# First attention of a Trainium2 kernel: two score passes interleaved unit by unit, row sums turned on TensorE, scores from two parts instead of three

## The chip, the cores and the metric

The kernel runs on one core of a Trainium2 chip. Its time is the device time of one execution in microseconds (us). TensorE multiplies matrices (PE is its multiply side, PEld its weight load), VectorE is DVE, ScalarE is ACT, GpSimd is POOL, and SyncE (SP) issues most DMAs.

## The reference

The whole is four transformer layers on x (8 batches, 256 rows, width 256), each an attention and a feed-forward sublayer after a layer norm. The change touches the first attention alone; q is the normalised x, k and v are a context of the same size.

```
qh = (q @ Wq.T + bq)  -> 16 heads of width 16      # kh, vh the same from the context
scores = einsum('bhqd,bhkd->bhqk', qh, kh) / sqrt(16)
scores = where(mask == 0, -1e10, scores);  attn = softmax(scores)
out = einsum('bhqk,bhkd->bhqd', attn, vh) -> (B, S, 256);  x = x + out @ Wo.T + bo
```

## The kernel before

The function `attention0` (lines 166 to 563) works batch by batch, eight batches of 256 rows. Each engine has its own program and waits on semaphores; PE runs its program in order. A unit `u` is two heads, so a batch has U = 8 units. Scores are formed twice. The first pass (`scores`, line 324) has queries on the partitions, and DVE takes the row maxima (`maxima`, line 517). The second pass (`weigh`, line 350) has keys on the partitions, takes the maxima in as further rows of the product, and ACT takes exp into `pT`; that is the layout in which the product with V needs it.

Full precision of the scores comes from three bf16 parts of q and of k (high, middle, low), stacked by DMA so that six products of parts are one contraction over 96 rows (`PARTS`, `to_stack`, line 223). SP issues the 12 DMAs for q and POOL the 12 for k; DVE makes the parts with ACT (`split`, `prepare`). The mask is added by a product of a bf16 identity with a tile of 0 or -2^100 (lines 340 and 365), one for each 128x256 piece of scores.

Both passes use the same four PSUM banks (0 to 3), two banks a unit, so they can't run at once. PE's order in a batch b (line 395) is: `project(b+1)` (q, k, v projections in fp32), `weigh(b)` in which unit u of the second pass alternates with the product of unit u-1 with V (line 376, four fp32 matmuls into 32 columns each, two column groups at a time), `scores(b+1)`, `spread_sums(b)`, `turn_maxima(b+1)`, `output(b)`. The softmax sums are a column of ones in V. `turn_sums` on SP moves them by DMA across the partitions, DVE inverts them (`reciprocals`), DMA moves them back into `rrow`, and a 128x128 selector product (line 384) spreads them over the partitions. DVE then multiplies (`onorm`, line 550), PE applies Wo, DVE adds to x (line 557).

The maxima go the way PE transpose (347), ACT, DVE, ACT, DVE (three parts, 457 to 532), three DMAs (263), and only then can `weigh` of that batch start. The loop is a hardware loop over pairs of batches (`every_batch`), with the last two batches written out.

Of the kernel before, what the change touches and what calls it, by code (L numbers as in the profile page):

```python
# [21 lines left out]
P = 128  # L22
# [143 lines left out]
def attention0(nc, top, x, xt, io, consts):  # L166

    G, NG, W = 4, H // 4, 32
    U = H // 2
    PARTS = ((0, 0, 0, 1, 1, 2), (0, 1, 2, 0, 1, 0))
    R = len(PARTS[0]) * D0  # L180
    LAND = 16 * 2 * len(PARTS[0])
    HB = P // D0
    with top.stage() as ctx:
        def sb(name, shape, dt=F32):
# [6 lines left out]
        sel = sb("sel", [P, P])  # L191
        ctxT = sb("ctxT", [P, 2, DK, S])
        mask, maskT = sb("mask", [P, TB, S], I32), sb("maskT", [P, TB, S], I32)
        neg, negT = sb("neg", [P, 2, TB, S], BF16), sb("negT", [P, 2, TB, S], BF16)
        part = sb("part", [P, 3, 2, DK, S], BF16)
        rest = sb("rest", [P, 2, DK, S])
        qs, ks = sb("qs", [P, 2, H, S], BF16), sb("ks", [P, 2, H, S], BF16)
        V = sb("V", [P, 2, TB, H, W])
        top_s = sb("top_s", [P, TB, H])
        mpart, mrest = sb("mpart", [H, 3, S], BF16), sb("mrest", [H, S])  # L200
        pT = sb("pT", [P, 2, 2, TB, S])
        sums, recip = sb("sums", [P, NG * S // W]), sb("recip", [P, NG * S // W])
        rrow = sb("rrow", [P, NG, S])
        oraw, onorm = sb("oraw", [P, NG, S]), sb("onorm", [P, NG, S])
        ps = ctx.enter_context(nc.psum_tensor("a0_ps", [P, 8, 512], F32))
        O = ps[:, 4:6, :].rearrange("p a (c n) -> p (a c) n", c=2)

        (weights, ctx_in0, ctx_in1, mask_in, ones_set, q_proj, k_proj, v_proj, hi_done, rest_done, mid_done, lo_done,
         stacked, v_out, neg_ready, s_ready, max_done, mt_ready, mhi_done, mrest_done, mmid_done, mlo_done,
         mrow_landed, st_ready, exp_done, pv_done, o_out, sums_landed, recip_landed, l_ready, recip_done, norm_done,  # L210
         wo_ready, resid_done) = (
             top.semaphore("a0_" + n) for n in (
                 "weights", "ctx_in0", "ctx_in1", "mask_in", "ones_set", "q_proj", "k_proj", "v_proj", "hi_done",
                 "rest_done", "mid_done", "lo_done", "stacked", "v_out", "neg_ready", "s_ready", "max_done",
                 "mt_ready", "mhi_done", "mrest_done", "mmid_done", "mlo_done", "mrow_landed", "st_ready",
                 "exp_done", "pv_done", "o_out", "sums_landed", "recip_landed", "l_ready", "recip_done", "norm_done",
                 "wo_ready", "resid_done"))
        gate, gate_set = sb("gate", [1, 4]), top.semaphore("a0_gate_set")
# [4 lines left out]
        def to_stack(engine, w, n, s):  # L223

            for t, which in enumerate(PARTS[w]):
                if which == n:
                    for k in range(DK):
                        engine.dma_start((qs, ks)[w][t * D0:(t + 1) * D0, s, k * HB:(k + 1) * HB, :],
                                         part[:, n, w, k, :]).then_inc((stacked, k_stacked)[w], 16)

        def every_batch(engine, body):

            with engine.Fori(0, B // 2 - 1) as pair:
                body(pair * 2, 0, pair, False)
                body(pair * 2 + 1, 1, pair, False)
            body(B - 2, 0, B // 2 - 1, False)
            body(B - 1, 1, B // 2 - 1, True)

        @block.sync
        def _(sp):  # L240
            sp.sem_inc(stacked, 16)
            sp.sem_inc(mrow_landed, 16)

            def load(b, s):
                sp.wait_ge(v_proj, b + 1)
                sp.dma_start(ctxT[:, s, :, :], io["ctxT"][bass.ds(b, 1)].rearrange("b (k p) s -> p (b k) s", p=P)
                             ).then_inc(ctx_in[s], 16)
                sp.wait_ge(neg_ready, b + 1)
                sp.dma_start(mask[:, :, :], io["mask"][bass.ds(b, 1)].rearrange("b (t p) s -> p (b t) s", p=P)
                             ).then_inc(mask_in, 16)  # L250
                sp.dma_start(maskT[:, :, :], io["maskT"][bass.ds(b, 1)].rearrange("b (t p) s -> p (b t) s", p=P)
                             ).then_inc(mask_in, 16)

            def stack(b, s):

                for n, ready in enumerate((hi_done, mid_done, lo_done)):
                    sp.wait_ge(ready, b * 2 + 1)
                    to_stack(sp, 0, n, s)

            def shift_rows(b, s):  # L260
                sp.wait_ge(mlo_done, b + 1)
                for n in range(3):
                    sp.dma_start(qs[R + n:R + n + 1, s, :, :], mpart[:, n, :]).then_inc(mrow_landed, 16)

            def turn_sums(b):

                sp.wait_ge(o_out, b * 2 + 2)
                for g in range(G):
                    sp.dma_start(sums[g * W:(g + 1) * W, :], oraw[g * W + D0:g * W + D0 + 1, :, :]
                                 ).then_inc(sums_landed, 16)  # L270
                sp.wait_ge(recip_done, b + 1)
                for g in range(G):
                    sp.dma_start(rrow[g * W + D0:g * W + D0 + 1, :, :], recip[g * W:(g + 1) * W, :]
                                 ).then_inc(recip_landed, 16)

            def feed(b, s):

                sp.wait_ge(pv_done, b * U + 2)
                stack(b + 1, 1 - s)
                turn_sums(b)  # L280
                shift_rows(b + 1, 1 - s)

            for dst, name in ((wq, "a0_wq"), (wk, "a0_wk"), (wv, "a0_wv"), (wo, "a0_wo")):
                sp.dma_start(dst[:, :, :], io[name].rearrange("k p n -> p k n")).then_inc(weights, 16)
            sp.dma_start(bqk[:, :, :], io["a0_bqk"]).then_inc(weights, 16)
            for dst, name in ((bv, "a0_bv"), (sel, "a0_sel")):
                sp.dma_start(dst[:, :], io[name]).then_inc(weights, 16)
            load(0, 0)
            load(1, 1)
            stack(0, 0)  # L290
            shift_rows(0, 0)
            with sp.Fori(0, B // 2 - 1) as pair:
                for s in range(2):
                    load(pair * 2 + (2 + s), s)
                    feed(pair * 2 + s, s)
            feed(B - 2, 0)
            turn_sums(B - 1)

        @block.tensor
        def _(pe):  # L300
            pe.sem_inc(v_proj, 2)
            pe.sem_inc(pv_done, 2)
            pe.sem_inc(l_ready, 1)
            pe.sem_inc(wo_ready, 1)
            pe.wait_ge(weights, 16 * 7)

            def project(b, s, half, left=1):
                pe.wait_ge(ctx_in[s], half * 16 + 16)
                pe.wait_ge(norm_done, left)
                for n, (w, src, done) in enumerate(((wq, xt, q_proj), (wk, ctxT, k_proj))):  # L310
                    for c in range(DK):
                        for k in range(DK):
                            mm = pe.matmul(ps[:, 6 + n, c * S:(c + 1) * S], w[:, k, c * P:(c + 1) * P],
                                           xt[:, k, bass.ds(b * S, S)] if src is xt else ctxT[:, s, k, :],
                                           start=(k == 0), stop=(k == DK - 1))
                    mm.then_inc(done, 1)
                pe.wait_ge(rest_done, b * 2 + 1)
                for t in range(TB):
                    for k in range(DK):
                        mm = pe.matmul(ps[:, 6, t * S:(t + 1) * S], ctxT[:, s, k, t * P:(t + 1) * P], wv[:, k, :],  # L320
                                       start=(k == 0), stop=(k == DK - 1))
                mm.then_inc(v_proj, 1)

            def scores(b, s, before):

                pe.wait_ge(stacked, (b + 1) * LAND + 16)
                pe.wait_ge(k_stacked, (b + 1) * LAND)
                pe.wait_ge(neg_ready, b + 2)
                pe.wait_ge(ones_set, 5)
                for u in range(U):  # L330
                    if u >= 2:
                        pe.wait_ge(max_done, b * U + (u - 1))
                    elif before is not None:
                        pe.wait_ge(exp_done, before * U + (U - 1 + u))
                    for j in range(2):
                        h, bank = 2 * u + j, ps[:, 2 * (u % 2) + j, :]
                        for t in range(TB):
                            pe.matmul(bank[:, t * S:(t + 1) * S], qs[0:R, s, h, t * P:(t + 1) * P], ks[0:R, s, h, :],  # L338
                                      start=True, stop=False)
# [1913 lines left out]
```

## Time and profile before

| | us |
|---|---|
| median of 3 runs (lowest, highest) | 2055.79 (2051.05, 2058.91) |
| the profiled execution's own time | 2057.15 |
| its span in the trace | 2055.3 |
| busy over the span: PE, PEld, DVE, ACT, POOL | 1573.8, 1345.9, 876.4, 550.3, 336.8 |

A row of the list of groups has line, engine, operation, output and input names, shapes, count, then busy time and mean ns of one, then the idle time of the engine before them with what released it. A busy time is the union of intervals; the duration of one matmul is longer than the distance from one to the next, since they are pipelined. In the timeline the first number is the start in us from the span's start, the second the length of the merged row.

### The profile page before, as it was taken

To read this page: it belongs to the slowest core of one execution; us is meant where nothing else is said; L and a number is where in the kernel's file an instruction comes from. 1 tells how busy PE (TensorE), PEld (TensorE's weight loads), DVE (VectorE), ACT (ScalarE), POOL (GpSimd) and SP (SyncE) were. 2 spreads that over 40 slices of the span, in tenths; PEclk is the share of its full clock that TensorE was granted. 3 is DMA by queue.
4 is the path that set the end of the run, shared out by engine and by line. 5 is a ranking of instruction groups with operands and counts; after the bars stand their busy time and mean duration, and the time that the engine had idled before them with its cause. 6 is when DMAs were issued, how large, how long until landed. Compare 5 with 4: busy or idle time off the path is not lost. (4 is left out here: it accounts for less than half of the span.)

```text
span 2055.3 us, 32700 instructions
## 1 busy us (share of the span) xinstructions
PE 1573.8 (77%) x11346; PEld 1345.9 (65%) x11346; DVE 876.4 (43%) x1913; ACT 550.3 (27%) x1311; POOL 336.8 (16%) x401
## 2 busy tenths in 40 slices
PE   2799997539991799999994099999999256691775
PEld 2565664429991688888874099999999244581664
DVE  5443542402224566665665011111111235448896
ACT  1233232102221455454441011111111011231553
POOL 1121120030002333332321400000000511004122
PEclk8999999569996799999995599999999678795787
DMA  4344241158132100000003454224470210101000
GB/s 127 59 76 66 48 69 12 59 200 276 39 113 86 61 7 7 7 7 2 2 1 113 148 195 148 103 67 146 148 270 18 76 47 16 34 26 41 6 15 21
DMA packets 118240, 152.13 MB, mean 74 GB/s; under 512 B 15360, under 2 KB 101376, under 8 KB 118016
## 3 DMA queue, kind: packets, MB, share of 16 engines
q1 hardware_dynamic: 101536, 123.86, 19.6%
q0 software_dynamic: 7680, 18.89, 4.1%
q10 hardware_dynamic: 8928, 8.13, 1.1%
q8 instruction: 56, 0.92, 0.2%
q14 instruction: 40, 0.33, 0.1%
HBM read 113.16 MB, written 24.64 MB: 67 GB/s over the span
## 5 line engine op out<-in xcount | busy, mean ns | idle before, releaser
L1271 PEld LDWEIGHTS f_ph<-f_xgT,f_w 128*128 128x128 f32 x3232 | 373.0, 193 | 21.7 <-issue 18.8
L1271 PE MATMUL f_ph<-f_xgT,f_w 128*128 128x128 f32 x3232 | 374.4, 277 | 16.1 <-DMA f_w<-in_f_w 14.9
L1281 PE MATMUL f_py<-f_w,f_hT 128*128 128x256 f32 x992 | 224.6, 379 | 0.0
L1281 PEld LDWEIGHTS f_py<-f_w,f_hT 128*128 128x128 f32 x992 | 183.7, 190 | 22.6 <-issue 0.2
L1342 DVE TENSOR_TENSOR f_hT<-f_ph,f_gate_o 128x512 f32<-128x512 f32 x78 | 54.0, 692 | 309.3 <-ACT f_gate_o L1305 309.3
L1376 POOL DMA_INDIRECT c_yt<-sorted_y,dest x48 | 45.6, 950 | 649.7 <-issue 648.8
L799 ACT ACTIVATE a_work<-a_ps,a_bias 128x128 f32<-128x128 f32 (+1 forms) x256 | 104.1, 419 | 149.0 <-DVE a_bias L879 91.3
L937 POOL TENSOR_TENSOR a_work<-a_work,a_recip 128x256 f32<-128x256 f32 (+1 forms) x128 | 103.1, 827 | 234.3 <-DVE a_recip L894 234.3
L145 PE MATMUL n_tp<-ident,n_xn 128*128 128x128 f32 x160 | 33.1, 384 | 134.9 <-DVE n_xn L125 134.3
L1305 ACT ACTIVATE f_gate_o<-f_ph 128x512 f32<-128x512 f32 x78 | 46.6, 597 | 295.2 <-PE f_ph L1271 295.1
L145 PEld LDWEIGHTS n_tp<-ident,n_xn 128*128 128x128 f32 x160 | 25.8, 196 | 142.7 <-DVE n_xn L125 135.9
L1260 PE MATMUL f_px<-ident,f_xg 128*128 128x128 f32 x124 | 24.3, 278 | 90.4 <-DMA f_xg<-sorted_x 90.4
L523 DVE TENSOR_REDUCE a_top_s<-a_ps 128x4 f32<-128x1024 f32 x64 | 75.7, 1215 | 16.4 <-PE a_ps L340 15.7
L899 DVE TENSOR_TENSOR a_qk<-a_ps,a_qk 128x512 fp32r<-128x512 f32 x64 | 44.3, 692 | 85.1 <-ACT a_qk L818 85.1
L467 ACT ACTIVATE a_pT<-a_ps 128x1024 f32<-128x1024 f32 x64 | 64.6, 1023 | 57.7 <-PE a_ps L365 57.7
L338 PE MATMUL a_ps<-a_ks,a_qs 96*128 96x256 bf16 x256 | 61.8, 279 | 22.3 <-DMA a_qs<-a_part 12.7
L1260 PEld LDWEIGHTS f_px<-ident,f_xg 128*128 128x128 f32 x124 | 15.7, 144 | 91.0 <-DMA f_xg<-sorted_x 91.0
L1173 POOL DMA_INDIRECT sorted_x<-xn,dest x48 | 46.4, 967 | 171.5 <-DVE dest L1149 157.5
L1349 DVE TENSOR_SCALAR f_hT<-f_ph,f_b 128x128 f32<-128x128 f32 x92 | 25.9, 345 | 111.5 <-PE f_ph L1271 111.5
L661 PE MATMUL a_ps<-a_src,a_wq_high 128*128 128x256 f32 x256 | 59.0, 312 | 17.4 <-DVE a_wk_low L843 14.6
L376 PE MATMUL a_ps<-a_pT,a_V 128*32 128x256 f32 x512 | 67.7, 385 | 2.8 <-ACT a_pT L467 1.8
L876 DVE TENSOR_REDUCE a_top_s<-a_ps 128x2 f32<-128x256 f32 (+1 forms) x128 | 64.4, 545 | 6.2 <-PE a_ps L724 6.2
(307 smaller groups left out, 3103.7 us busy)
## 6 DMA issues: line engine op xcount, KB each, us to landing
f_w<-in_f_w SPq DMA_DIRECT2D x72, 1024.0 KB, 7.2
f_xg<-sorted_x SPq DMA_DIRECT2D x62, 128.0 KB, 2.1
sorted_y<-f_yg ACTq DMA_DIRECT2D x62, 128.0 KB, 1.7
a_qs<-a_part SPq DMA_DIRECT2D x96, 64.0 KB, 5.1
a_ks<-a_part POOLq DMA_DIRECT2D x96, 64.0 KB, 5.3
sorted_x<-zeros SPq DMA_DIRECT2D x1, 4992.0 KB, 16.5
a_ctxT<-in_ctxT SPq DMA_DIRECT2D x16, 256.0 KB, 2.7
sorted_x<-zeros SPq DMA_DIRECT2D x1, 2944.0 KB, 10.2
```

The lines of the kernel that those rows point to most:

```text
L145: mm = pe.transpose(tp[:, b % SLOTS, k, t * P:(t + 1) * P], xn[:, row if router else row % (SLOTS * TB), k * P:(k + 1) * P], ident[:, :])
L338: pe.matmul(bank[:, t * S:(t + 1) * S], qs[0:R, s, h, t * P:(t + 1) * P], ks[0:R, s, h, :], start=True, stop=False)
L376: mm = pe.matmul(O[W * (g0 + j):W * (g0 + j + 1), n, :], V[:, s, t, 4 * n + g0 + j, :], pT[:, m % 2, j, t, :], start=(t == 0), stop=(t == ...
L467: act.activation(pT[:, u % 2, :, :, :].rearrange("p j t n -> p j (t n)"), ps[:, 2 * (u % 2):2 * (u % 2) + 2, :], ACT.Exp, scale=float(D0) ...
L523: dve.tensor_reduce(top_s[:, :, 2 * u:2 * u + 2].rearrange("p t j -> p j t"), ps[:, 2 * (u % 2):2 * (u % 2) + 2, :].rearrange("p j (t k) - ...
L661: mm = pe.matmul(out, left[a][c], right[b][c], start=start and i == 0, stop=stop and i == len(todo) - 1)
L799: act.activation(prob[:, s, i, t * P:(P if t == 0 else TRI)], ps[:, SB + 2 * s + i, t * S:(t * S + P * (t + 1))], ACT.Exp, bias=bias[:, s, ...
L876: dve.tensor_reduce(top_s[:, s, t, :], ps[:, SB + 2 * s:SB + 2 * s + 2, t * S:t * S + P * (t + 1)], AX.X, ALU.max).then_inc(max_done, 1)
L937: pool.tensor_tensor(part, part, recip[:, s, t, :].unsqueeze(2).to_broadcast([P, 2, P * (t + 1)]), ALU.mult).then_inc(shares_done, 1)
L1271: mm = pe.matmul(ph[:, q, n, f * P:(f + 1) * P], w[:, s, k, (q * FQ + f) * P:(q * FQ + f + 1) * P], xgT[:, s, k, :], start=(k == 0), stop= ...
L1281: mm = pe.matmul(py[:, s, 0:D], hT[:, s, f, :], w2[:, s, f, :], start=(f == 0), stop=(f == FT - 1))
L1342: dve.tensor_tensor(hT[:, s, q * FQ:(q + 1) * FQ, :].rearrange("p f n -> p (f n)"), ph[:, q, 1, :], gate_o[:, q, :], ALU.mult).then_inc(h_ ...
```

## The change

- The loop is gone: every engine runs through `steps`, k from -16 to 69, with i = k // 8 and u = k % 8. In step k PE forms unit k of the second pass (banks 0 and 1, `ST`) and unit k+9 of the first (banks 2 and 3, `SC`; units 0 to 8 use both pairs of banks by turns). The other work of the batches i+2 (projections, stacking), i+1 (maxima), i (product with V) and i-1 (sums, output) has a fixed u.
- q and k have two fp32r parts, the contraction is 48 rows (50 in the second pass), and the two heads of a unit stand in rows 0 to 63 and 64 to 127. The DMAs are 6 for q and 6 for k, of fp32. The maxima have two parts and four DMAs. Buffers by batch (`qs`, `ks`, `V`, `neg`, `negT`) are three instead of two.
- The product with V is made for two units at once, four heads in four column groups.
- The sums are turned by products with a 128x4 selector, inverted from PSUM, widened by a POOL copy and transposed on PE, with no DMA. `gate` on POOL goes. Weights are waited for in three lots.

```
+    HALF, ROWS = P // 2, 3 * D0
+    AHEAD = U + 1
+    PARTS = ((0, 0, 1), (0, 1, 0))
+    ST, SC, OB, MB = 0, 2, 4, 6
+        part = sb("part", [P, 2, 2, DK, S], F32R)
+            def shut(first, which, b):
+                for j in range(2):
+                    for t in range(TB):
+                        pe.matmul(ps[:, first + j, t * S:(t + 1) * S], consts["identb"][:, :], which[:, b % 3, t, :], ...)
+            def pairs(first, left, right, rows, b, u):
+                for t in range(TB):
+                    for j in range(2):
+                        r = slice(j * HALF, j * HALF + rows)
+                        mm = pe.matmul(ps[:, first + j, t * S:(t + 1) * S], left[r, b % 3, u, t * P:(t + 1) * P],
+                                       right[r, b % 3, u, :], start=False, stop=True, skip_group_check=True)
+            def scores(k):
+                m = k + AHEAD
...                       # waits neg_ready at a batch's start
+                    pe.wait_ge(max_done, m)          # from m = 9 on
+                    shut(bank(m), neg, m // U)
+                    pe.wait_ge(exp_done, k)
+                    shut(ST, negT, k // U)
...                       # at a batch's start: q_stacked, k_stacked
+                    pairs(bank(m), qs, ks, ROWS, m // U, m % U).then_inc(s_ready, 1)
...                       # at a batch's start: mrow_landed
+                    pairs(ST, ks, qs, ROWS + 2, k // U, k % U).then_inc(st_ready, 1)
+            def weigh(b, n):
+                pe.wait_ge(exp_done, b * U + (2 * n + 2))
+                if n == 0:
+                    pe.wait_ge(recip_done, b)        # and v_out, mlo_done
+                for t in range(TB):
+                    for g in range(G):
+                        mm = pe.matmul(O[W * g:W * (g + 1), n, :], V[:, b % 3, t, G * n + g, :],
+                                       pT[:, n % 2, g, t, :], start=(t == 0), stop=(t == TB - 1))
+            def turn_sums(b):                        # 8 products, 4 moving columns each
+                        mm = pe.matmul(ps[:, OB, c:c + G], oraw[:, n, t * P:(t + 1) * P], sel[:, :], ...)
+            def spread_sums(b):                      # 8 transposes of wide
+            for k in steps:
+                i, u = k // U, k % U
+                scores(k)
+                if u == 0: queries(i + 2); turn_sums(i - 1)
+                if u == 1: keys(i + 2)
+                if u == 3: spread_sums(i - 1)
+                if u in (2, 4, 6): weigh(i, u // 2 - 1)
+                if u in (4, 5): output(i - 1, u - 4)
+                if u == 6: turn_maxima(i + 1)
+                if u == 7: values(i + 2); weigh(i, NG - 1)
```

(The PE loop stands here in short form; each call is made where its batch exists.) DVE in step k: `maximum(k+9)`, then by u: 0 low part of q, 1 low part of k and `reciprocals(i-1)`, 2 both masks of i+2, 3 `normalise(i-1)`, 4 copy out of half of O, 5 residual of i-1, 6 low part of the maxima, 7 V bias and the other half of O. ACT: exp of unit k, then the high part of q (u 0), of k (u 1), of the maxima (u 6). POOL sets all of `ks` to 1 first, stacks k, and makes `widen(i-1)` (128x1024) behind the stacking of k.

## Rows read from the trace of the kernel before

**Rows 1.** Busy time by stretch (us, instructions), granted clock, DMA share, GB/s

```profile
108.00:146.70 38.70, 36.46 (x246) 23.90 (x245) 18.89 (x27) 12.97 (x17) 6.65 (x15) 1.00 0.40 64
690.00:1050.00 360.00, 343.22 (x3200) 300.52 (x3198) 225.43 (x493) 176.00 (x629) 112.84 (x133) 0.99 0.02 5
```

**Rows 2.** Timeline around one batch, PE, ACT and SP

```profile
103.59 0.38 PE L347 MATMUL a_ps<-ident,a_top_s 128*16 128x128 f32 x2
104.09 0.37 ACT L457 ACTIVATE a_mpart<-a_ps 16x256 bf16<-16x256 f32 x1 [12.78 <-PE a_ps L347]
...
105.83 1.77 SPq L263 DMA_DIRECT2D a_qs<-a_mpart  x3
108.11 1.89 PE L313 MATMUL a_ps<-xt,a_wq 128*128 x8
109.83 1.89 PE L313 MATMUL a_ps<-a_ctxT,a_wk 128*128 128x256 f32 x8
113.67 0.27 PE L363 MATMUL a_ps<-a_qs,a_ks 99*128 99x256 bf16 x1
...
141.52 0.37 ACT L457 ACTIVATE a_mpart<-a_ps 16x256 bf16<-16x256 f32 x1 [12.65 <-PE a_ps L347]
```

**Rows 3.** Timeline of one unit of the second pass, PE

```profile
81.93 0.27 PE L363 MATMUL a_ps<-a_qs,a_ks 99*128 99x256 bf16 x1
82.04 0.27 PE L365 MATMUL a_ps<-a_negT,identb 128*128 128x256 bf16 x1
82.25 1.06 PE L376 MATMUL a_ps<-a_pT,a_V 128*32 128x256 f32 x8
83.24 0.28 PE L363 MATMUL a_ps<-a_qs,a_ks 99*128 99x256 bf16 x1
```

**Rows 4.** Groups of this stage, 29 to 372 us

```profile
L523 DVE TENSOR_REDUCE a_top_s<-a_ps 128x4 f32<-128x1024 f32 x64 | 75.7, 1215 | 16.4 <-PE a_ps L340 15.7
L467 ACT ACTIVATE a_pT<-a_ps 128x1024 f32<-128x1024 f32 x64 | 64.6, 1023 | 57.7 <-PE a_ps L365 57.7
L447 ACT ACTIVATE a_part<-a_ps,a_bqk 128x256 bf16<-128x256 f32 x32 | 13.4, 470 | 44.0 <-PE a_ps L313 44.0
...
L499 DVE SCALAR_TENSOR_TENSOR a_rest<-a_ps,a_bqk,a_part 128x256 f32<-128x256 f32 x32 | 14.0, 480 | 13.7 <-ACT a_part L447 13.7
L515 DVE RECIPROCAL a_recip<-a_sums 128x32 f32<-128x32 f32 x8 | 2.8, 346 | 3.7 <-DMA a_sums<-a_oraw 3.6
```

**Rows 5.** Timeline of another attention (fp32r), PE

```profile
702.74 0.82 PE L704 MATMUL a_ps<-ident,a_work 128*128 128x128 f32 x6
703.39 0.39 PE L717 MATMUL a_ps<-tri,identb 128*128 128x128 bf16 x4
703.71 0.97 PE L724 MATMUL a_ps<-a_qk 64*128 64x256 f32 x12
704.61 1.20 PE L661 MATMUL a_ps<-a_wv_high,a_src 128*128 128x512 f32 x4
```

**Rows 6.** Groups on POOL, another stage

```profile
L1490 POOL COPY f_xb<-xt 128x512 f32 x8 | 5.1, 649 | 39.3 <-PEq L1494 26.0 <-PE f_po L1503 13.3
```

**Rows 7.** DMA issues of this stage: count, KB each, median us to landing

```profile
a_ks<-a_part POOLq DMA_DIRECT2D x96, 64.0 KB, 5.3
a_qs<-a_mpart SPq DMA_DIRECT2D x24, 8.0 KB, 1.8
```

**Rows 8.** Timeline of the start and of the end of the stage

```profile
37.35 3.35 PE L313 MATMUL a_ps<-xt,a_wq 128*128 128x256 f32 x8 [9.48 <-DMA a_ctxT<-in_ctxT]
...
57.61 0.40 PE L338 MATMUL a_ps<-a_ks,a_qs 96*128 96x256 bf16 x1 [12.74 <-DMA a_qs<-a_part]
...
76.11 0.28 PE L363 MATMUL a_ps<-a_qs,a_ks 99*128 99x256 bf16 x1
...
333.49 0.28 PE L363 MATMUL a_ps<-a_qs,a_ks 99*128 99x256 bf16 x1 [0.55 <-DMA a_qs<-a_mpart]
...
349.86 0.69 DVE L541 COPY a_oraw<-a_ps 128x512 f32<-128x512 f32 x1 [6.44 <-PE a_ps L376]
...
369.06 0.69 DVE L557 TENSOR_TENSOR x<-a_ps,x 128x512 f32<-128x512 f32 x1 [6.26 <-PE a_ps L391]
```

More of the change, by code:

```diff
@@ L231, in every_batch @@
[L231 to L237, printed above, removed]
+                    for j in range(DK):
+                        engine.dma_start((qs, ks)[w][j * HALF + t * D0:j * HALF + (t + 1) * D0, b % 3, :, :].bitcast(F32),
+                                         part[:, n, w, j, :].bitcast(F32)).then_inc((q_stacked, k_stacked)[w], 16)
@@ L239, in _ @@
+        steps = range(-2 * U, B * U + 6)
         @block.sync
         def _(sp):
[L241 to L252, printed above, removed]
@@ L288, in _, with load_ctx @@
[L288 to L297, printed above, removed]
+            def load_ctx(b):
+                if b >= 2:
+                    sp.wait_ge(v_proj, b - 1)
+                sp.dma_start(ctxT[:, b % 2, :, :], io["ctxT"][b].rearrange("(k p) s -> p k s", p=P)
+                             ).then_inc(ctx_in[b % 2], 16)
@@ new lines, in high, with exps @@
+            def high(b, n, proj, done):
+                act.wait_ge(proj, b + 1)
+                if b >= 1:
+                    act.wait_ge((q_stacked, k_stacked)[n], b * LAND)
+                for c in range(DK):
+                    a = act.activation(part[:, 0, n, c, :], ps[:, MB + n, c * S:(c + 1) * S], ACT.Identity,
+                                       bias=bqk[:, n, c:c + 1])
+                a.then_inc(done, 1)
+            def exps(k):
+                b, u = k // U, k % U
+                act.wait_ge(st_ready, k + 1)
+                if k >= 4:
+                    act.wait_ge(pv_done, k // 2 - 1)
+                act.activation(pT[:, u // 2 % 2, 2 * (u % 2):2 * (u % 2) + 2, :, :].rearrange("p j t n -> p j (t n)"),
+                               ps[:, ST:ST + 2, :], ACT.Exp, scale=float(D0) ** -0.5).then_inc(exp_done, 1)
@@ L473, in _ @@
-            split(0, first=True)
-            split_maxima(0)
-            every_batch(act, batch)
+                if b >= 1:
+                    act.wait_ge(mrow_landed, b * 64)
+                act.mul(mpart[:, 0, :], ps[0:H, OB, 0:S], -1.0).then_inc(mhi_done, 1)
+            for k in steps:
+                i, u = k // U, k % U
+                if is_unit(k):
+                    exps(k)
+                if u == 0 and is_batch(i + 2):
+                    high(i + 2, 0, q_proj, q_high)
+                if u == 1 and is_batch(i + 2):
+                    high(i + 2, 1, k_proj, k_high)
+                if u == 6 and is_batch(i + 1):
+                    split_maxima(i + 1)
```

528 lines of the change are left out of this document (270 added, 258 removed).

## Prediction, made before the changed kernel was run

> **What bounds the kernel now.** The first view to read is the table of busy time by stretch [rows 1]. In a middle batch of the stage (108.0 to 146.7 us) PE is busy 36.46 of 38.70 us at a granted clock of 1.00, while DVE has 18.89 and ACT 12.97. The second is the timeline: the same instruction (L457) starts at 104.09 and at 141.52, so a batch takes 37.43 us [rows 2]. The stage runs from PE's first product at 37.35 to the last DVE add at 369.06 + 0.69 = 369.75 [rows 8]. PE does its program in order, so PE's order and what it waits for set the end. The list of groups shows what is alternated instead of overlapped: DVE's 64 maxima cost 75.7 us and fall in the first pass, ACT's 64 exps cost 64.6 us and fall in the second, where ACT idled 57.7 us for PE [rows 4]. Nothing of the stage runs beside a later stage, so what a batch saves the kernel saves.
>
> **What PE's pieces cost.** From one start to the next:
> - A bf16 product of 256 columns takes 0.11 (81.93 to 82.04) [rows 3].
> - A change between full products and column groups adds about 0.09: 82.04 to 82.25 is 0.21 [rows 3].
> - fp32 projections: eight records in 1.72 (108.11 to 109.83), 0.215 each [rows 2].
> - Product with V: eight records in two column groups take 82.25 to 83.24, 0.99 with its exit [rows 3].
> - fp32r products in two row groups: 12 records from 703.71 to 704.61, 0.90, and 0.15 from the last bf16 record to the first of them where 0.06 would be its pace [rows 5]. Six pairs, so a pair costs 0.12, and entry, exit and a slower first pair 0.28 together. Four pairs make 0.48 + 0.28, about 0.77.
> - 128x128 fp32 loads for short products: six in 703.39 - 702.74 = 0.65, 0.108 each [rows 5].
>
> **The change, a step of one unit.** Removed: 16 products of parts over 96 or 99 rows and the alternation. Kept: 8 mask products, 8 x 0.1125 = 0.90. Added: 8 fp32r records in four pairs, 0.77. So S = 1.67 us for both passes of a unit. I take the pair's price at 48 rows from the row at 64 rows, as the nearest. Its other end is one after the other, 0.12 a record, +0.48 a step.
>
> The product with V for four heads is 16 records in four groups. If four groups run as two did, it is four rounds of 0.215 and a change, 0.95. The other end is two at a time, 1.72 + 0.1 = 1.82. I take 0.95 since the two-group row keeps its full pace in each group. The skill speaks against it here. The Trainium skill (TensorE: Matmul & The Clock Gate, Part 3) says that a weight load overlaps a running product only where the row groups differ, and column groups share all rows. By that rule the loads would stand between the rounds. The trace disagrees for two groups, since eight loads and eight records fit in 0.99 where the records alone, two by two, need 0.86.
>
> DVE's cycle gives a floor. A maximum takes 1.225 [rows 4]; then PE must be told (0.05), put 0.90 of mask products and the entry and first pass's two pairs before it (0.31), and the last record must drain (0.28 + 0.05): 2.82 us between two maxima, since banks 2 and 3 hold one unit at a time. A step is thus S plus its other PE work, at least 2.82.
>
> Steps of a middle batch, in us:
> - u 0: q projection 1.72, turning the sums 16 x 0.107 = 1.71: 5.10. It replaces four DMAs each way and costs no wait.
> - u 1: k projection: 3.40.
> - u 2: V product 0.95. The k values reach ACT 0.2 after PE (two high parts, 13.4 / 16 = 0.84), then DVE (two low parts, 14.0 / 16 = 0.88, and hand-offs of 0.1, reciprocal 0.35) [rows 4], so the next maximum starts at 5.75 from the start of u 1 and ends at 6.97; PE's next mask waits for it: 3.65.
> - u 3: transposes 8 x 0.108 fit in the floor: 2.82. Their POOL copy of 1024 columns is two of 649 ns [rows 6], 1.3, and POOL issues two DMAs before it, 1.05; it ends near 7.8 and PE wants it at 8.7.
> - u 4: V product and half of the output, 0.95 + 1.72: 4.35. u 5: 3.40.
> - u 6: V product, then the transposes of the maxima, behind this step's maximum: 2.82 + 0.22 = 3.05.
> - u 7: v projection and V product: 4.35.
>
> The sum is 30.1, and I take 30.2 against 37.43. The moved waits: the maxima's chain is now PE 103.59 to the last landing near 105.83 + 1.2 + 1.8 = 108.8 [rows 2, 7]. Two links go (0.9), one DMA comes (0.6), so 4.9. It is covered by u 7 (4.35) and 1.2 of the next step's masks and first pass, by 0.6 us only; if that cover fails, each microsecond is paid 6 times. Stacking ends near 6.5 + 5.3 (landing) = 12 from the start of u 1 [rows 7], and u 7 wants it at 21. SP passes no wait in front of it that is open later than u 2. DMA bytes stay, the descriptors are 1 KB instead of 512 B.
>
> **The whole stage.** Start: the stage waits for three weight DMAs instead of seven, 3 us less than 37.35, and six q DMAs instead of twelve end some 4 us sooner, so the first pass starts near 49 instead of 57.61 [rows 8]. There DVE has 9.8 us for eight maxima, and batch 1's low parts, masks and the V bias (3.3), with hand-offs and a cold first 3 us: the maxima are turned near 68 and landed near 73. Before, the second pass started at 76.11. Step 0 then counts from 71.7. Batch 0 has no sums and no output of an earlier batch: 26.0. Batches 1 to 5: 151. Batch 6 has no projections and no first pass in its last step, but its maxima's chain is uncovered by 2.6: 27.2. Batch 7 has no first pass; its unit is bound by exp (1.02) with half the masks and two pairs, 2.16, and by the rest: 20.9. Tail, in place of 349.86 to 369.75 (20 us): copy 0.69, turn 1.7, reciprocal 0.35, POOL 1.3, transposes 0.9, multiply 1.4, output 3.5 to 6, add 0.69 and hand-offs: 13.5. Sum: 71.7 + 26.0 + 151 + 27.2 + 20.9 + 13.5 = 310.3, against 369.75: **59.5 us less**. The parts: 4.4 at the start, 333.49 - 76.11 = 257.4 against 204.2, and 36.3 against 34.4.
>
> The profiled execution took 2057.15; it becomes 1997.7. It lies 1.4 above the median of the three runs, so I forecast 1996. POOL's memset of `ks` (6144 columns), unshown here, is bounded by DVE's 0.89 and POOL's copy at 1.27 ns a column, 5.5 to 7.8 us; it begins at 29.4 and k's high part comes after 40, so both ends cost nothing. Unrolling adds no executed work; whether code arrives in time no row tells, and I leave 5 us above for it.
>
> A second rule: the Trainium skill (TensorEngine Tiling (Array Packing), Key Properties) says that changing the tiling mode drains TensorE. A full drain would be 0.27 less 0.11, so 0.16 instead of 0.09 a change, by rows 3, and some 20 changes a batch would make 11 us more. The rows decide for 0.09, without a drain of the whole length.
>
> **Rivals.**
> 1. *V products only two at a time.* +0.87 each: nearly all of it in u 4 and u 7, 0.7 in u 6, 0.6 in u 2 (behind the wait for the reciprocal): 3.0 a batch, 24 in all, 2020. For it: no row shows four groups. Against it: two run at full pace.
> 2. *Hand-offs.* Each step a further 0.4 us, since masks of the second pass stand in front of the first pass's pairs and any late ACT or DVE delays both: 3.2 a batch, about +26, 2022. For it: the cover of 0.6 us above, and DVE's work between maxima.
> 3. *Pairs not side by side at 48 rows*: +0.48 x 64 = 31, less what the floor hides in u 3: 2026. Against it: rows 5 at 64 rows.
> 4. *No interleaving in effect*: a batch waits about 5 us for the maxima's DMAs at its start, 8 x 5 = 40: 2036. Speaks for it: at that point PE has no other work in its order.
> 5. *Slower:* PE works mostly at 1.2 GHz in this stage, half the clock. About 27 us of PE work in a batch would take 54; 8 x 26 = 208 more, about 2200. It decides from some 60 of those 208, that is where three tenths of the stage falls to the lower level. Against it: the fp32r stage ran at 0.99 with the same pairs [rows 1], and PE here is at 1.00 with more idle time than it would have.
>
> **Chances.** Forecast 0.63 (its own range 1978 to 2012), rival 1 0.13, rival 2 0.11, rival 3 0.05, rival 4 0.04, rival 5 0.04. From 1976 to 2034 all but about 0.1 is in: the low end is a batch at PE's bare work (27.9, 18 less), the high end holds rivals 1 to 3 alone and some of their sums. A measurement of this kernel tells 0.5%, 10 us, from no change. Rivals 1 to 3 are all beyond that: faster 0.94, the same 0.02, slower 0.04.
>
> **What would show it.** A batch's period of 30.2 between two first high parts of the maxima, and 2.8 between maxima in u 3. V products of 16 records from start to next work in 0.95 (1.8 for rival 1); pairs of fp32r records starting within 10 ns (0.12 apart for rival 3); PE idle before the second pass's first unit of a batch (under 1 us, or 5 for rival 4); the clock 1.00 (rival 5). Nothing after the stage should change in length. It is wrong if the stage's last add ends later than 325 us after the span's start, or before 289.

## The result, and the profile after

The changed kernel takes 2019.45 us (median of 4 runs, 2016.12 to 2022.42) against 2053.42 for the kernel before beside it; the ratio is 0.9833 [0.9801, 0.9865]. The forecast was 1996 with 1976 to 2034 around it: the sign and the wide range hold. The likeliest case's own range (1978 to 2012) doesn't. The time stands where rivals 1 and 2 were priced (2020 and 2022), and neither of them is what happened, so that it lies in the wide range is luck in the main. In profiled executions 2057.15 became 2016.12, 41.0 us less where 59.5 were forecast.

The stage's last add now ends at 331.26 + 0.69 = 331.95, where it was 369.75 [rows 8] and should have been 310.3. The prediction said that it is wrong if this add ends later than 325; by that sign of its own it is. What lies behind the stage became 3.2 us shorter with the same work, and differs by more than that between executions of one kernel.

Busy time by stretch of the changed kernel (columns as in [rows 1]): start, end of the start, a middle batch, batch 7 with the tail.

```profile
29.00:70.00 41.00, 20.25 (x88) 14.62 (x88) 13.77 (x20) 3.36 (x8) 12.07 (x13) 0.71 0.73 131
70.00:100.00 30.00, 23.21 (x165) 15.96 (x166) 15.00 (x19) 8.46 (x11) 3.31 (x7) 0.77 0.75 101
111.80:142.80 31.00, 29.45 (x259) 22.06 (x259) 16.84 (x23) 10.25 (x13) 4.22 (x7) 1.00 0.53 79
294.70:332.00 37.30, 30.91 (x200) 21.30 (x200) 6.14 (x10) 8.16 (x8) 2.08 (x2) 0.77 0.00 0
```

The middle batch stands at full clock with PE busy 29.45 of 31.00. Before, 36.46 of 38.70 [rows 1]: PE bounds as it did, with less work and without less idle share. The other stretches have a clock of 0.71 to 0.77.

The batch's period, between two first high parts of the maxima (timeline, ACT):

```profile
167.66 0.37 ACT L498 ACTIVATE a_mpart<-a_ps 16x256 fp32r<-16x256 f32 x1 [0.44 <-PE a_ps L364]
...
198.63 0.37 ACT L498 ACTIVATE a_mpart<-a_ps 16x256 fp32r<-16x256 f32 x1 [0.44 <-PE a_ps L364]
```

30.97 us, where it was 37.43 [rows 2] and 30.2 was forecast. The wait in brackets is 0.44 instead of 12.78 [rows 2]: ACT is no longer parked through a first pass.

Timeline of steps 2 to 4 of another middle batch:

```profile
212.60 0.50 PE L328 MATMUL a_ps<-a_ks,a_qs 48*128 48x256 f32 x4
...
212.94 0.40 PE L328 MATMUL a_ps<-a_qs,a_ks 50*128 50x256 f32 x4
213.25 3.17 POOL L226 DMA_DIRECT2D a_ks<-a_part  x6 [26.75 <-ACT a_part L482]
...
213.99 1.07 PE L382 MATMUL a_ps<-a_pT,a_V 128*32 128x256 f32 x16 [0.65 <-DVE a_recip L569]
215.00 0.61 PE L321 MATMUL a_ps<-a_neg,identb 128*128 128x256 bf16 x4
...
216.41 1.05 POOL L464 COPY a_wide<-a_recip 128x1024 f32<-128x1024 f32 x1
...
217.52 1.09 PE L411 MATMUL a_ps<-ident,a_wide 128*128 128x128 f32 x8 [0.80 <-POOL a_wide L464]
...
220.08 1.07 PE L382 MATMUL a_ps<-a_pT,a_V 128*32 128x256 f32 x16
221.08 1.99 PE L420 MATMUL a_ps<-a_wo,a_onorm 128*128 128x256 f32 x8
```

Read it for three things. Four fp32r records (two pairs) take 0.34 to the next group, where 0.31 was priced. A V product of 16 records takes 1.00 (220.08 to 221.08), where eight took 0.99 [rows 3]. And PE waits at two places: 0.65 for the reciprocal, and 0.80 for POOL's copy, which starts when POOL has issued all six of k's DMAs.

The start (timeline), and where its DMAs landed (issues from 29 to 86: count, KB each, median us to landing):

```profile
33.00 3.78 PE L288 MATMUL a_ps<-xt,a_wq 128*128 128x256 f32 x8 [5.39 <-DMA a_wk<-in_a_wk]
...
37.75 4.03 SPq L226 DMA_DIRECT2D a_qs<-a_part  x6
...
41.34 3.66 POOL L226 DMA_DIRECT2D a_ks<-a_part  x6 [6.96 <-ACT a_part L482]
...
55.80 0.79 PE L328 MATMUL a_ps<-a_ks,a_qs 48*128 48x256 f32 x4 [12.77 <-DMA a_ks<-a_part]
...
76.69 2.88 SPq L259 DMA_DIRECT2D a_qs<-a_mpart  x4
...
80.08 0.80 PE L328 MATMUL a_ps<-a_ks,a_qs 48*128 48x256 f32 x4 [3.42 <-DMA a_ks<-a_part]
80.81 3.33 PE L313 MATMUL a_ps<-a_wv,a_ctxT 128*128 128x256 f32 x8
...
85.73 1.02 ACT L491 ACTIVATE a_pT<-a_ps 128x1024 f32<-128x1024 f32 x1 [8.22 <-PE a_ps L328]
```

```profile
a_qs<-a_part SPq DMA_DIRECT2D x12, 128.0 KB, 4.6
a_ks<-a_part POOLq DMA_DIRECT2D x12, 128.0 KB, 8.6
```

PE starts 4.35 sooner than before, where 3 was forecast, and then waits 12.77 for k's stack. ACT takes batch 0's turned maxima at 75.84, and SP issues their four DMAs from 76.69 on; by the semaphore events of the trace the last of them landed at 82.2. Meanwhile PE stands before unit 8, batch 1's first, which the lookahead puts in front of batch 0's second pass. It waits 3.42 for batch 1's stack and starts at 80.08, and 3.3 of v projection follow at the lower clock. The first exp comes at 85.73.

The end (timeline) with the windows row of 9 us of it, and then windows of a stretch of 15 us before it in a further execution of the changed kernel (columns as in [rows 1]):

```profile
294.12 0.50 PE L328 MATMUL a_ps<-a_qs,a_ks 50*128 50x256 f32 x4 [1.24 <-DMA a_qs<-a_mpart]
294.55 3.03 PE L395 MATMUL a_ps<-a_sel,a_oraw 128*128 128x4 f32 x16
...
318.77 0.69 DVE L562 COPY a_oraw<-a_ps 128x512 f32<-128x512 f32 x1 [4.56 <-PE a_ps L382]
...
325.77 5.46 PE L420 MATMUL a_ps<-a_wo,a_onorm 128*128 128x256 f32 x16 [0.78 <-DVE a_onorm L576]
331.26 0.69 DVE L583 TENSOR_TENSOR x<-a_ps,x 128x512 f32<-128x512 f32 x1 [5.55 <-PE a_ps L420]
```

```profile
296.00:305.00 9.00, 7.88 (x46) 4.49 (x48) 0.36 (x1) 2.05 (x2) 1.04 (x1) 0.50 0.00 0
```

```profile
266.00:269.00 3.00, 3.00 (x25) 2.63 (x24) 1.04 (x1) 1.02 (x1) 0.00 (x0) 0.79 0.00 0
269.00:272.00 3.00, 2.10 (x13) 1.33 (x12) 1.49 (x2) 1.02 (x1) 0.07 (x1) 0.50 0.00 0
272.00:275.00 3.00, 3.00 (x20) 1.89 (x22) 0.68 (x1) 0.25 (x1) 0.98 (x1) 0.50 0.02 5
...
278.00:281.00 3.00, 2.94 (x27) 2.10 (x25) 2.26 (x3) 1.03 (x1) 0.00 (x0) 1.00 0.00 0
```

The 16 sum products take 2.90 here from their start to the next row (297.45): in the trace they start 0.11 apart until the clock falls at 295.2, and 0.21 apart behind it. The 16 records of the output take 5.46, 0.43 apart and then 0.216, the pace at full clock.

### The profile page after: what moved, and what is told of

It is laid out like the page before. It is cut to its first block and busy times, and to the rows that moved or that the text cites. A ratio compares the mean times of both kernels' runs of the same rounds, so it can differ in the third digit from the quotient of the medians.

```text
span 2014.0 us, 32419 instructions
## 1 busy us (share of the span) xinstructions
PE 1536.6 (76%) x11506; PEld 1343.2 (67%) x11506; DVE 858.2 (43%) x1886; ACT 536.7 (27%) x1285; POOL 323.9 (16%) x337
## 5 line engine op out<-in xcount | busy, mean ns | idle before, releaser
L1317 PEld LDWEIGHTS f_ph<-f_xgT,f_w 128*128 128x128 f32 x3232 | 374.3, 194 | 21.7 <-issue 17.9
L1351 ACT ACTIVATE f_gate_o<-f_ph 128x512 f32<-128x512 f32 x78 | 46.6, 597 | 295.2 <-PE f_ph L1317 295.1
L750 PE MATMUL a_ps<-ident,a_work 128*128 128x128 f32 x384 | 53.7, 277 | 15.4 <-POOL a_work L983 7.9
L770 PE MATMUL a_ps<-a_qk 64*128 64x256 f32 x768 | 63.7, 299 | 0.0
```

The costliest lines, as they stand in the source:

```text
L750: mm = pe.transpose(ps[:, TB_ + i, n * P:(n + 1) * P], prob[:, s, i, n * P:(n + 1) * P], consts["ident"][:, :])
L770: mm = pe.matmul(ps[:, SB + 2 * s + i, t * S:(t + 1) * S], qk[r, s, a, 0, t * P:(t + 1) * P], qk[r, s, b, 1, :], start=False, stop=(n == l ...
L1317: mm = pe.matmul(ph[:, q, n, f * P:(f + 1) * P], w[:, s, k, (q * FQ + f) * P:(q * FQ + f + 1) * P], xgT[:, s, k, :], start=(k == 0), stop= ...
```

## The experiments

Each is the changed kernel with one edit, unless said otherwise. Times are medians; a ratio is to the kernel before measured beside it, with its 95% interval. A middle batch's period is read as above.

**The changed kernel again**, measured beside two of the three groups of experiments (the loads, the v projections, the copy and the three edits together have no repeat beside them).

> The changed kernel itself, beside the experiments on the same chip. Expected 2017 to 2022 us, a batch's period of 31.0 us, second pass starting near 85.7 us after the span's start.

> The changed kernel again, beside the next three on one chip: 2013 to 2020 us, first exp near 85.5 us, period 31.0.

2014.77 (0.9792 [0.9769, 0.9815]) and 2013.91 (0.9786 [0.9769, 0.9802]); period 30.97 in both; first exp at 85.1 and 87.1. The start varies by 2 us between executions, the period doesn't. The stage ends at 332.05 and 334.0.

**Order inside the V product.**

```
-  for t in range(TB):
-      for g in range(G): mm = ...
+  for g0 in (0, 2):
+      for t in range(TB):
+          for g in (g0, g0 + 1): mm = ...
```

> The changed kernel with the V product of four heads made as two groups, then the other two. Theory A (the four-group product is the largest part of a batch's gain): each of the 32 products takes 1.82 instead of 1.0 us; 3.0 us a batch by the same steps as in the prediction's rival 1, +24 us, about 2043, period 34. Theory B (interleaving is what gained, and PE has slack that hides the product): under +8 us.

2014.85, 0.9798 [0.9774, 0.9823]: no change. In the trace four records still start within 0.04 us of one another (213.921, .927, .951 and .958), and all 16 take 1.02 (213.92 to 214.94), although the edit lists groups 2 and 3 behind all records of 0 and 1. The records don't name their column group; that four groups run side by side is read from these times. The edit didn't halve the width, so it prices nothing. Width had to be taken away by other work in between (below).

**The kernel before, with only the V product over four heads** (exp buffer for four heads, V products after units 3, 5, 7 and at the end).

```
-  if u > 0: ...
-      for j in range(2): O[W*(g0+j)...] V[...] pT[:, m % 2, j, t, :]
+  if u in (3, 5, 7, 8): ...
+      for g in range(G): O[W*g...] V[...] pT[:, n % 2, g, t, :]
```

> The kernel before with one part of the change alone: the V product for four heads in four column groups, behind every second unit of the second pass, pT with four heads a buffer. Theory A: 4 products of 1.0 in place of 8 of 0.99 us a batch, the period falls from 37.43 to about 33.5, -31 us, about 2022: most of the gain without any interleaving. Theory B: PE then waits for exp (2.04 a pair of units against 1.8 + 1.0 of PE work leaves little), the period falls by 1 to 1.5 only, about -10 us.

2029.09, 0.9867 [0.9844, 0.989], 28 us less than before, where 31 was expected. Its windows row of one batch, and its timeline:

```profile
147.20:180.50 33.30, 31.05 (x241) 21.65 (x239) 18.08 (x26) 11.37 (x17) 6.73 (x16) 1.00 0.43 73
```

```profile
124.98 0.27 PE L338 MATMUL a_ps<-a_ks,a_qs 96*128 96x256 bf16 x1 [1.33 <-DMA a_ks<-a_part]
...
169.83 0.37 ACT L457 ACTIVATE a_mpart<-a_ps 16x256 bf16<-16x256 f32 x1 [12.67 <-PE a_ps L347]
...
203.09 0.37 ACT L457 ACTIVATE a_mpart<-a_ps 16x256 bf16<-16x256 f32 x1 [12.67 <-PE a_ps L347]
```

The period is 33.26 here and in half of the batches; in the others it is 34.3 to 34.6, of which 1.0 to 1.3 is a wait for a stack (the line at 124.98). So 2.9 to 4.2 of the 6.5 us a batch come from this product alone, with the passes still one after the other (ACT waits its 12.67).

**The changed kernel's pieces without interleaving**: all first passes of a batch, then its second passes, two bank pairs taking turns in each.

```
-  scores(k)                       # unit k+9 and unit k together
+  if is_unit(k): second(k)
+  if u == 7: for m in batch i+1: first(m); turn_maxima(i + 1)
```

> The changed kernel without the interleaving: all pieces stay (fp32r pairs, four-group V product, sums on PE), but the second pass of a batch runs through first, both passes use both pairs of banks by turns, and the first pass of the next batch follows as a block, then the maxima, the v projection and the next q and k projections. Theory A: PE's work of a batch is 28.7 us, the block of maxima is bound by DVE (8 x 1.225 = 9.8 against 6.7 of PE), so +3 and a few hand-offs: period 33.5 to 34, +20 to +25 us, about 2042. Theory B: interleaving carries the gain: period 36 or more, 2055 or more. If it is under 2025, interleaving is worth nothing here.

2063.33, 1.0031 [1.0015, 1.0048], 48.6 us above the changed kernel, about twice the expected price. Not all of it is in the stage: in the profiled execution the stage's last add ends at 368.53, 36.6 later than in the changed kernel (34.5 later than in its slowest repeat), and the other 11 us lie behind the stage, where the work is the same; why isn't known. Timeline, and windows of one batch:

```profile
180.58 0.37 ACT L496 ACTIVATE a_mpart<-a_ps 16x256 fp32r<-16x256 f32 x1 [12.30 <-PE a_ps L359]
...
218.07 0.37 ACT L496 ACTIVATE a_mpart<-a_ps 16x256 fp32r<-16x256 f32 x1 [12.09 <-PE a_ps L359]
```

```profile
142.70:152.00 9.30, 9.30 (x51) 7.83 (x50) 2.06 (x5) 2.13 (x6) 0.00 (x0) 0.86 0.25 46
152.00:170.40 18.40, 16.47 (x153) 10.38 (x152) 5.11 (x10) 8.06 (x8) 4.18 (x7) 1.00 0.81 108
170.40:180.50 10.10, 7.77 (x59) 4.64 (x60) 9.43 (x8) 0.00 (x0) 0.00 (x0) 0.95 0.01 2
```

The period is back at 37.49, in other batches 36.3 to 38.1. In the block of first passes (third row) DVE is busy 9.43 of 10.10: the lighter scores no longer cover the maxima. Each pass also pays entry and exit of the row pairs for itself (0.28, an estimate of 2.2 a batch), and the clock is 0.86 and 0.95 in two of the stretches. How the 6.5 us divide among these wasn't measured.

**The later loads moved ahead of q's stacking** (wv, bv, wo, sel and batch 1's context issued first).

```
+  sp.dma_start(wv ...); sp.dma_start(bv ...); load_ctx(1); sp.dma_start(wo ...); ...
   for i in range(-2, B):
       if is_batch(i + 2): stack(i + 2)
-      if i == -2: (the same five)
```

> The changed kernel with the loads of wv, bv, the second context, wo and sel issued at the stage's start, before the stacking of batch 0 instead of behind it. Theory A (the first pass starts late since 1.1 MB of these loads share the DMA engines with the stacking of k): the DMA engines are free from 34.7 to 39 us and take them there; k's last part, issued near 45, lands after 5.3 as in other batches, near 50.5 instead of 55.8: -5 us. Theory B (the stacking's own 1.5 MB takes that long): -1 us or nothing.

2017.36, 0.9803 [0.9763, 0.9842]; the first pass starts at 54.05 (54.03 and 55.48 in the repeats) and the first exp comes at 85.7, as without the edit. The explanation by the weights' transfers falls.

**v projections of batches 0 and 1 ahead of the waits** for their stacks.

```
+  if k in (-AHEAD, -1): values(i + 2)      # and not at u == 7
   scores(k)
```

> The changed kernel with the v projections of batches 0 and 1 placed in PE's order ahead of the first pass's unit that waits for stacking (steps -9 and -1), in place of behind it. Theory A (PE's in-order waits of 12.8 and 3.4 us stand in front of work that is ready): 3.5 us of cold projection and 3.3 us go under the waits, -6 to -7 us. Theory B (what follows is bound by DVE's maxima or by the maxima's DMAs anyway): under -2.

2014.26, 0.9791 [0.9773, 0.9808]. The first exp comes at 81.3, some 4 to 6 sooner, where 6 to 7 was expected; the period is 30.97. The stage ends at 328.28, 4 to 6 sooner as well. The gain shows in the trace and is too small for the medians.

**POOL's copy ahead of its stacking, DVE's reciprocals ahead of k's low part.**

```
-  stack(i + 2); widen(i - 1)
+  widen(i - 1); stack(i + 2)
-  low(i + 2, 1, k_high, k_low); reciprocals(i - 1)
+  reciprocals(i - 1); low(i + 2, 1, k_high, k_low)
```

> The changed kernel with the reciprocals ahead of the low part of k on DVE, and POOL's widening copy ahead of the stacking of k. Theory A (in every middle batch PE waits 0.65 us for the reciprocal in step 2 and 0.8 for POOL's copy in step 3): step 2 loses 0.35, step 3 0.6, the period falls from 31.0 to about 30.0, -6 us in all. Theory B (DVE's cycle takes the place of the waits): the period falls by under 0.3, -2 us.

2013.82, 0.978 [0.9758, 0.9802]. Timeline:

```profile
167.77 0.37 ACT L498 ACTIVATE a_mpart<-a_ps 16x256 fp32r<-16x256 f32 x1 [0.44 <-PE a_ps L364]
...
197.88 0.37 ACT L498 ACTIVATE a_mpart<-a_ps 16x256 fp32r<-16x256 f32 x1 [0.45 <-PE a_ps L364]
```

The period is 30.11. Step 2 takes 3.15 and step 3 takes 2.81, the floor that the prediction worked out (2.82). So both waits in the timeline above come from these two orders. The median is that of the repeats (2013.9 and 2014.8): five periods give 4.3 us, but in the profiled execution the first exp comes late, at 87.6, and the stage ends at 331.1, under 1 us before the changed kernel.

**The three edits together.**

> The three edits together (early loads, v projections under the waits, reciprocals and widening first). If they add up: -5, -6.5 and -6, about -17 us against the changed kernel, near 1999, the first exp near 73 us after the start instead of 85.5 and the period 30.0. If the early loads already take the wait that the v projection is put under, part of the first two counts once: -13.

2009.89 (2008.14 to 2012.49), 0.977 [0.9752, 0.9788], the lowest median, where 1999 was expected. First exp 82.0, period 30.1, and the stage ends at 324.2, 7.8 sooner than in the changed kernel. Against the changed kernel the medians differ by 4 to 5 us, and the intervals of the ratios overlap with those of its repeats. The start's two waits in it:

```profile
53.87 0.80 PE L327 MATMUL a_ps<-a_ks,a_qs 48*128 48x256 f32 x4 [9.10 <-DMA a_ks<-a_part]
...
76.81 0.79 PE L327 MATMUL a_ps<-a_ks,a_qs 48*128 48x256 f32 x4 [3.74 <-DMA a_ks<-a_part]
```

The first wait is shorter only because the v projection now stands in front of it: the first pass starts at 53.87, as in the faster repeat (54.03). The second wait stays.

**V products in two halves with other PE work between them**, so that two column groups run at a time.

```
-  weigh(i, n)                      # 16 records
+  weigh(i, n, 0); ...; weigh(i, n, 1)   # 8 and 8, apart
```

> The changed kernel with each V product of four heads cut into two of two heads, with other PE work between them (step 2 and step 3; before and behind the output in step 4, the maxima's transposes in step 6 and the v projection in step 7), so that only two column groups can run at once. The same 32 records pairs by pairs: each half takes 0.96. Theory A (the four-group product is worth what the prediction put on it, 0.87 each where PE is the bound): +0.2 in step 3, +0.96 in steps 4, 6 and 7, period near 34, about +25 us. Theory B (PE has slack): under +8 us.

2036.9, 0.9893 [0.9877, 0.991], 23 us above the changed kernel. Timeline:

```profile
163.82 1.06 PE L382 MATMUL a_ps<-a_pT,a_V 128*32 128x256 f32 x8
...
164.81 1.99 PE L421 MATMUL a_ps<-a_wo,a_onorm 128*128 128x256 f32 x8
...
174.42 0.37 ACT L505 ACTIVATE a_mpart<-a_ps 16x256 fp32r<-16x256 f32 x1 [0.45 <-PE a_ps L364]
...
208.65 0.37 ACT L505 ACTIVATE a_mpart<-a_ps 16x256 fp32r<-16x256 f32 x1 [0.45 <-PE a_ps L364]
```

Eight records take 0.99 (163.82 to 164.81), as sixteen do in the changed kernel; the period is 34.23. That is rival 1's case made by hand: it gave +3.3 a batch where the rival said 3.0, and +23 where it said 24.

**Stacks of two parts**: leaves out the products of q's high with k's low parts; 32 rows instead of 48 in the first pass, 34 instead of 50 in the second, and four DMAs instead of six for each stack.

```
-  HALF, ROWS = P // 2, 3 * D0
-  PARTS = ((0, 0, 1), (0, 1, 0))
+  HALF, ROWS = P // 2, 2 * D0
+  PARTS = ((0, 1), (0, 0))
```

> The changed kernel without the third product of parts (q high with k low is left out; contraction over 32 rows, and 8 stacking DMAs of 128 KB a batch instead of 12). PE's steps don't change (a pair of 32 rows costs what one of 48 does), so the period stays 31.0. Theory A (the start is bound by the DMA engines moving the stack's own bytes, 1.5 MB in 11.5 us): 1.0 MB takes 7.7, the first pass starts near 51 instead of 55.5 and step -1 no longer waits 3.4 us for batch 1's stack: first exp near 78, -7 us. Theory B (issue and landing time of the last DMA bound it): two DMAs fewer in POOL's row, -1 us, first exp 84 or later.

2020.51 (2013.47 to 2024.52), 0.9804 [0.9779, 0.983]. The first exp comes at 80.3, but the period is 31.8 instead of 31.0, which the expectation excluded. Windows and timeline:

```profile
143.50:175.30 31.80, 31.07 (x259) 22.47 (x260) 18.07 (x23) 10.26 (x14) 3.14 (x5) 1.00 0.29 60
175.30:208.70 33.40, 32.67 (x259) 23.57 (x260) 18.02 (x23) 10.22 (x14) 3.14 (x5) 0.95 0.29 57
```

```profile
184.98 0.50 PE L328 MATMUL a_ps<-a_ks,a_qs 32*128 32x256 f32 x4
...
185.41 0.50 PE L328 MATMUL a_ps<-a_qs,a_ks 34*128 34x256 f32 x4
```

From the first pass's pairs to the second's it is now 0.43 instead of 0.34, and PE is busier (31.07) with fewer rows. The 0.09 is what a change between full products and column groups cost, so I read it as a change of the array's division between 32 and 34 rows that 48 and 50 rows don't need; the trace shows the time and not the reason. It makes 0.7 a batch. The next batch takes 33.4 at a granted clock of 0.95, and batch 0 takes 31.4 (26.1 in the changed kernel) at 0.84: in this execution the clock fell in two batches where it stood at 1.00 in the others, and that took back what the start had gained. First stacks a third smaller left the first pass at 53.44, 0.6 to 2.4 sooner than in the three executions of the changed kernel.

**A further order at the start**: copy, reciprocal and v edits, and unit 8 moved behind batch 0's first second pass.

```
+  if k == 0: scores(0, first=False); scores(-1)
+  ...queries(i + 2); scores(0, second=False)
```

> The changed kernel with the v projections of batches 0 and 1 under the stacking waits, reciprocals and widening first, and the first pass's first unit of batch 1 moved behind unit 0 of the second pass (steps -1 and 0 in PE's order), so that batch 0's exp no longer waits for batch 1's stack. By the rows of the runs before: -4 (first exp 81.3), -5 to -6 (period 30.1) and a further -2.6 when step 1's masks start at 81.4 instead of 84.0: -12 against the changed kernel, 2003 to 2006. If the deferred unit only moves the wait into step 0 and 1, the third part is nothing: -9.5.

2010.52, 0.9778 [0.9756, 0.9801], as with the three edits; 2003 to 2006 was expected. The first exp comes at 79.8, 5 to 7 sooner than the changed kernel's, but step 0 then takes 9.88 and the second exp comes at 89.7. Timeline:

```profile
79.00 0.80 PE L328 MATMUL a_ps<-a_qs,a_ks 50*128 50x256 f32 x4 [5.81 <-DMA a_qs<-a_mpart]
...
81.42 3.78 PE L288 MATMUL a_ps<-xt,a_wq 128*128 128x256 f32 x8
...
87.96 0.61 PE L321 MATMUL a_ps<-a_neg,identb 128*128 128x256 bf16 x4 [1.33 <-DVE a_top_s L556]
```

PE no longer waits for batch 1's stack. It waits 5.81 for the maxima's DMAs, and then does unit 8, the q projection (3.78, twice its time at full clock), unit 9 and a wait of 1.33 for the maximum before the second exp. The maxima landed 7.9 after ACT took them, where a middle batch needs 4.9.

The landings in the traces say why. In the ten executions in which batch 1's stack of twelve DMAs is on its way meanwhile, the maxima land 2.0 to 2.3 us after that stack's last DMA and 6.4 to 8.0 after ACT took them. In the two in which it isn't (two parts: landed at 72.2 before the maxima were turned; without interleaving: issued later), they land after 5.0 and 5.2. So at the start the maxima's DMAs seem to be held up until batch 1's stack has landed; no run moved that stack alone.

## Why the prediction was right or wrong

The forecast's stage end was 310.3, measured was 331.95. The 21.7 us divide as follows, by the first exp of each batch:

| part | forecast | measured | more |
|---|---|---|---|
| first exp of batch 0 | 73.0 | 85.7 | 12.7 |
| batch 0 | 26.0 | 26.1 | 0.1 |
| batches 1 to 5 | 151 | 154.9 | 3.9 |
| batch 6 | 27.2 | 28.0 | 0.8 |
| batch 7 and tail, from its first exp | 33.1 | 37.3 | 4.2 |

(33.1 is 34.4 less 1.3 from a step's start to its exp.) The rest of the kernel gave 3.2 back, and 59.5 - 21.7 + 3.2 is the 41.0 of the profile.

**The step that failed: the start.** "Six q DMAs instead of twelve end some 4 us sooner, so the first pass starts near 49 instead of 57.61", and "the maxima are turned near 68 and landed near 73". The 4 us took the number of DMAs for what sets the landing, while the bytes stay, and k's stack had no term. In the traces the issuing of q's did get shorter by that, 3.4 from first to last instead of 7.2. But the landings of both stacks come 1.27 apart for 128 KB, where they came 0.46 apart for 64 KB, and from the first issue to the last landing 17.9 went by (37.75 to 55.66) instead of 14.6 (42.99 to 57.57). So of PE's earlier start only 1.9 was left, and the first pass started at 55.80, 6.8 late.

The other 5.9 of the 12.7 are three terms. The first pass to the turned maxima (ACT at 75.84) took 20.0 instead of 19. The maxima's DMAs landed 6.4 after that instead of 5, behind batch 1's stack. And the first exp came 3.5 after that landing, at once in the forecast: PE's order has unit 8 and a v projection at the lower clock in front of unit 0's second pass, and the prediction gave this order no term, though the lookahead of nine units is in its own reading of the code. Unit 8's wait itself ended at 80.08, before the maxima had landed (82.2), and cost nothing; the projection and step 0's masks behind it held PE until 85.3. With the v projections moved the first exp comes 1.5 after the landing. Why the first stack lands so late isn't settled. It isn't the later loads alone (no change when moved), and a third fewer bytes gave at most 2.4. POOL's and SP's queues were not exchanged.

**The middle** is right in its mechanism, and its sum is so close partly because errors cancel. Steps by exp to exp, measured against forecast: 5.17 (5.10), 3.46 (3.40), 3.37 (3.65), 3.44 (2.82), 4.47 (4.35), 3.47 (3.40), 3.01 (3.05), 4.57 (4.35). One is off by over 0.3: u 3. POOL issues six DMAs before the copy, where the prediction counted two (it took k's high parts as issued long before). The swap of orders gave 2.81 and a period of 30.1, the forecast 30.1 to 30.2. But the forecast had the late reciprocal in its 3.65 for u 2, where the swap leaves 3.15: 0.5 too much there makes up for 0.5 too little in the other steps.

Three numbers of the working don't come out, and the sum doesn't hang on them: a maximum is 1.215 in [rows 4], not 1.225; the scores removed are 8 products of parts a unit (256 in each pass of 64 units), not 16; and PE's bare work of a batch adds up to 28.6 by the prediction's own prices, not 27.9, so the low end of the range was a little too low.

**V product.** 0.95 was forecast and 1.00 measured, with 16 records. The rule of the Trainium skill (TensorE: Matmul & The Clock Gate, Part 3) quoted against it is not borne out: 16 weight loads and 16 records of four column groups take the same 1.0 as 8 and 8 of two, so the loads hide although all groups share the rows (in the trace a load of 0.11 starts 2 ns behind a product and ends before the next round of products, 0.215 later). The run with halves apart shows that the width is what is paid for.

**Mode changes** at 0.09 hold: the steps above are sums with it. The Trainium skill (TensorEngine Tiling (Array Packing), Key Properties) says that a change drains TensorE. A drain of the full length was worked out at +11 in all, 1.4 a batch; the six steps other than u 2 and u 3 exceed their forecast by 0.5 together, so the trace speaks against it.

**Rivals.** 1 refuted and its price confirmed (+23 against +24). 2: hand-offs are small; at most 0.5 a batch by the same sum, where the rival said 3.2. 3 refuted: records of a pair start within 4 ns of one another and 0.12 behind the pair before. 4 refuted in the middle: the cover for the maxima's DMAs, thin by the working, held in every middle batch: they land 0.8 to 1.2 before the batch's first exp. At the start a wait of its kind is real, as told above. 5: the middle is at 1.00, the ends are not; over the whole stage the granted clock is 0.90, where it was 0.95 before, so less than the three tenths at the lower level that the rival asked for.

**End.** Batches 6 and 7 were priced at full clock. In the repeated execution the windows show the clock at 0.79 and then 0.50 (1.2 GHz) from 266 on, with PE busy 3.00, 2.10 and 3.00 of 3.00; before the fall it did masks, pairs and the sum products of four moving columns. It is back at 1.00 by 278. Batch 6's first three steps take 4.76, 3.94 and 4.22 there, and 3.45, 2.81 and 2.80 in the execution with the reordered V product, whose clock fell later. By the same comparison the lower clock cost the first changed execution 1.4 in batch 6 and 1.4 in step 0 of batch 7. The tail came out: from the copy at 318.77 to the last add's end are 13.2, forecast 13.5. So what batch 7 and the tail have too much lies in batch 7, from its first exp to that copy 24.1 instead of 19.6. Its first three steps (4.56, 2.88 and 3.52) fall in the stretch at 0.50 and the next is 2.17, as forecast (2.16). How the 4.5 divide beyond the 1.4 is open, since no execution had batch 7 at full clock. The maxima's chain is not in it, with 1.24 of wait for 2.6 forecast.

**Interleaving.** The prediction gave one sum for all. The runs divide it: the four-head V product alone makes 28 of some 42 us. The remainder is fp32r pairs, sums turned on PE and interleaving together. With the pieces of the changed kernel, taking the interleaving out costs 48.6, of which 35 to 37 are in the stage; that DVE then bounds one pass is part of it. These two numbers don't add, because the old pieces in phases (2029) beat the new ones in phases (2063). So the 48.6 is the price of this one order in phases; whether a better one with the new pieces would come closer wasn't tried.

## What to carry to other kernels

Price a stage's start and end by themselves: write down PE's order there, lookahead units too, and take landing times from a stretch with as full queues. The same bytes in half as many DMAs halved the issuing of q's stack (3.4 us instead of 7.2) and shortened nothing up to the last landing. And look at what else is on its way when a small transfer is waited for: here the maxima's came in only behind the large ones issued before them. Before crediting a reordering, try the densest single piece alone: here products with 32 columns of output, four abreast, made two thirds of the gain in the old order. Where two passes load different engines, interleaving pays once the passes are light enough for the other engine to bound one of them, as DVE did here (9.43 of 10.10). And name the parts of a sum in the check: the total lay in the range here while the start was 12.7 us off.

## What was unexpected

- Column groups listed two by two within one block still ran four abreast by the times, starting within 0.04 us.
- Going from products over 32 rows to products over 34 costs 0.09; from 48 to 50 nothing. Shorter products made the batch 0.8 longer.
- The maxima's four DMAs of 8 KB took 4.9 us from ACT to landing in middle batches and 6.4 to 8.0 at the start, always ending 2.0 to 2.3 behind batch 1's stack.
- The clock fell to 1.2 GHz around and behind the sum products, once in a window in which PE's records were busy 3.00 of 3.00 (266 to 269); why isn't shown. These products are loads of 128x128 weights for four moving columns, and they start 0.11 us apart at full clock and 0.21 at the lower one.
